# Turned maxima copied by ScalarE instead of VectorE, and the second mask product cut to its 64 non-zero columns

## The reference, cut to what matters

```
q, k, v = proj(wq), proj(wk), proj(wv)      # 32 heads of width 16
q, k = rope(q), rope(k)
scores = q @ k.T / sqrt(16)
scores = where(causal, scores, -inf)
attn = softmax(scores)                      # over the keys
out = attn @ v                              # then @ wo
```

## Time and profile before

| what | value |
|---|---|
| median of 3 runs | 857.84 us (856.75 to 858.73) |
| profiled execution, its span (no other time is shown for it) | 855.8 us |
| PE, DVE, ACT, POOL busy | 92%, 74%, 50%, 36% of the span |
| maxima (line 1614) | x320, 182.7 us busy on DVE |
| copies of the turned rows (line 1621) | x16, 402 ns median |
| mask products (line 734) | x512, 59.0 us busy on PE |
| attention with both kinds of scores | about 438 to 642 us of the span |

### The profile page before, as it was taken

One profiled execution on the slowest core, in us unless ns is written; L12 is line 12 of the kernel. 1 busy time (PEld: TensorE's weight loads), 2 busy tenths in 40 slices (PEclk: granted clock), 3 DMA queues, 4 the chain that ended last, 5 costly groups with the idle time before them and its releaser, 6 DMA issues.

```text
span 855.8 us, 18987 instructions
## 1 busy us (share of the span) xinstructions
PE 790.1 (92%) x7930; PEld 377.1 (44%) x7930; DVE 633.1 (74%) x895; ACT 427.9 (50%) x576; POOL 304.4 (36%) x217
## 2 busy tenths in 40 slices
PE   7668797797999999999989999999998999999997
PEld 2434343444444444544434444444435544444444
DVE  4999999998555333444569999999976787774344
ACT  4986557554844330143225777787784633332100
POOL 0699899993003000055530222212233222221000
PEclk9599899999999999999979999999998999999999
DMA  6900000005230000056640000000132023320001
GB/s 217 375 3 2 3 3 3 3 3 172 99 108 10 1 0 1 1 80 118 121 76 2 2 2 1 2 2 2 48 131 64 1 79 127 130 84 0 13 37 50
DMA packets 53297, 46.63 MB, mean 54 GB/s; under 512 B 38290, under 2 KB 44242, under 8 KB 53219
## 3 DMA queue, kind: packets, MB, share of 16 engines
q1 hardware_dynamic: 53218, 45.49, 18.6%
HBM read 34.87 MB, written 2.16 MB: 43 GB/s over the span
## 4 chain that ended last, share of the span: by engine, by line
PE 69%; DVE 16%; issue 5%; POOL 5%; ACT 3%; DMA 1%; SPq 1%; DVEq 0%; POOLq 0%; ACTq 0%
PE ps L870 13%; PE ps L651 10%; PE ps L628 8%; DVE arena L1388 8%; PE ps L805 8%; PE ps L906 7%; PE ps L730 6%; PE ps L707 6%; PE ps L789 3%; POOL arena L1238 3%; DVE arena L1614 2%; PE ps L734 2%; PE ps L542 2%; PE ps L498 1%; ACT arena L1147 1%
## 5 line engine op out<-in xcount | busy, mean ns | idle before, releaser
L1614 DVE TENSOR_REDUCE arena<-ps 128x1 f16<-128x512 f32 (+3 forms) x320 | 182.7, 630 | 11.1 <-PE ps L730 4.9
L1147 ACT ACTIVATE arena<-ps 128x1024 f32<-128x1024 f32 (+2 forms) x160 | 142.2, 942 | 54.4 <-PE ps L789 53.6
L1238 POOL TENSOR_TENSOR arena<-arena 128x1024 f32<-128x1024 f32 x62 | 152.0, 2487 | 9.4 <-DVE arena L1388 8.9
L1388 DVE TENSOR_TENSOR_SCAN arena<-arena,ps 128x1024 f32<-128x1024 f32 x64 | 142.0, 2268 | 1.4 <-PE ps L542 1.1
L870 PE MATMUL ps<-arena 128*128 128x512 f16 x528 | 114.6, 379 | 0.1
L730 PE MATMUL ps<-arena 64*128 64x512 f16 (+3 forms) x384 | 100.0, 337 | 4.5 <-DVE arena L1614 1.8
L651 PE MATMUL ps<-arena 128*128 128x512 f16 (+1 forms) x464 | 97.6, 372 | 1.0 <-ACT arena L1071 1.0
L1288 POOL TENSOR_SCALAR_AFFINE_SELECT arena<-arena 128x512 f32<-128x512 f32 x64 | 42.5, 669 | 155.4 <-ACT arena L1147 155.3
L996 ACT ACTIVATE arena<-arena,negA 128x1024 f32<-128x1024 f32 x64 | 72.9, 1147 | 45.4 <-DVE arena L1388 43.6
L542 PE MATMUL ps<-arena 64*128 64x64 f16 x3072 | 60.6, 196 | 35.8 <-DVE arena L1388 32.1
L542 PEld LDWEIGHTS ps<-arena 64*128 64x128 f16 x3072 | 52.8, 99 | 86.3 <-DVE arena L1388 79.3
(11 more groups left out here) (173 smaller groups left out, 964.6 us busy)
## 6 DMA issues: line engine op xcount, KB each, us to landing
arena<-in_w_q_dram SPq DMA_DIRECT2D x11, 768.0 KB, 4.3
arena<-c_rows SPq DMA_DIRECT2D x16, 512.0 KB, 11.2
arena<-in_w_s_dram SPq DMA_DIRECT2D x11, 384.0 KB, 4.8
arena<-in_x_fm_dram SPq DMA_DIRECT2D x8, 256.0 KB, 4.1
out_dram<-arena SPq DMA_DIRECT2D x8, 256.0 KB, 2.0
arena<-in_wg_dram SPq DMA_DIRECT2D x1, 1792.0 KB, 10.0
arena<-in_wu_dram SPq DMA_DIRECT2D x1, 1792.0 KB, 7.3
arena<-in_wd_dram SPq DMA_DIRECT2D x1, 1792.0 KB, 11.3
```

Of the source, the lines that this page charges most:

```text
L1147: nc.scalar.activation(dst, src, ACT.Exp, scale=float(HD) ** -0.5).then_inc(exp_done, 1)
L1238: nc.gpsimd.tensor_tensor(hC[i % 4][:], hst[i % 3][:], c_all[:, n, :], ALU.mult).then_inc(hc_done, 1)
L1388: nc.vector.tensor_tensor_scan(hst[i % 3][:], dA[i % 3][:], banks(2 * (i % 2), 2), 0.0, ALU.mult, ALU.add).then_inc(scan_done, 1)
L1614: nc.vector.reduce_max(maxima_slot(half, k), ps[:, ring_bank(n), 0:len(heads) * w].rearrange("p (a w) -> p a w", a=len(heads)), AX, negate ...
```

## The change

ScalarE takes over `keep_rows`, under a count of its own, `rows_kept`. `ring_read` then counts only what VectorE reads, so every wait on it is renumbered (`read_to`), and TensorE's wait for a bank whose last unit was a turn is a wait on `rows_kept`. The second mask product runs over 64 columns instead of 128.

```diff
+        ROWS_AT = {EARLY_TURN} | {RING_AT[step] for step in IN_RING if step[0] == "turn"}
+        def read_to(n):
+            return n + 1 - sum(at <= n for at in ROWS_AT)
+        def rows_to(n):
+            return sum(at <= n for at in ROWS_AT)
...
             def put_rows(g, half):
-                sp.wait_ge(ring_read, RING_AT["turn", g, half] + 1)
+                sp.wait_ge(rows_kept, rows_to(RING_AT["turn", g, half]))
...
             def ring_slot(n):
-                if EARLY <= n < EARLY + RING:
-                    pe.wait_ge(ring_read, EARLY)
-                elif n >= EARLY + RING:
-                    pe.wait_ge(ring_read, n - RING + 1)
-                elif n >= 2:
-                    pe.wait_ge(ring_read, n - 1)
+                before = EARLY - 1 if EARLY <= n < EARLY + RING else n - 2 if n < EARLY else n - RING
+                if before in ROWS_AT:
+                    pe.wait_ge(rows_kept, rows_to(before))
+                elif before >= 0:
+                    pe.wait_ge(ring_read, read_to(before))
                 return ring_bank(n)
...
                     if diag:
-                        for s in range(2):
-                            last = nc.tensor.matmul(dst[:, w - P:w], picks_b[rows, s, :], mask_b[rows, s, :], start=False, stop=(s == 1))
+                        for s, cols in ((0, P), (1, SUB)):
+                            last = nc.tensor.matmul(dst[:, w - cols:w], picks_b[rows, s, :], mask_b[rows, s, P - cols:P], start=False, stop=(s == 1))
...
+            def keep_rows(g, half, n):
+                act.wait_ge(ring_full, n + 1)
+                if g:
+                    act.wait_ge(m_rows[half], 32 * g)
+                nc.scalar.copy(m_row[0:GH, half * HALF:(half + 1) * HALF], ps[0:GH, ring_bank(n), :].bitcast(f16)[:, 0:HALF]).then_inc(rows_kept, 1)
             for t in range(TT):
                 stack(t)
+                if t == 5:
+                    keep_rows(0, 0, EARLY_TURN)
...
                     e += 1
+                elif kind == "turn":
+                    keep_rows(g, half, RING_AT[kind, g, half])
                 elif kind == "keep":
                     keep_out(g, half)
...
-            def keep_rows(g, half, n):
-                dve.wait_ge(ring_full, n + 1)
-                if g:
-                    dve.wait_ge(m_rows[half], 32 * g)
-                nc.vector.tensor_copy(m_row[0:GH, half * HALF:(half + 1) * HALF], ps[0:GH, ring_bank(n), :].bitcast(f16)[:, 0:HALF]).then_inc(ring_read, 1)
...
-                elif kind == "turn":
-                    keep_rows(g, half, RING_AT[kind, g, half])
```

More of the change, by code:

```diff
@@ L182, in build @@
         m_joined, r_made = sem("m_joined"), sem("r_made")
+        rows_kept = sem("rows_kept")
         m_rows = [sem("m_rows0"), sem("m_rows1")]
@@ L281, in searched @@
                 return len(SEARCH[0])
-            return max([RING_AT["search", g, half, k] for k in range(len(SEARCH[half])) if ("search", g, half, k) in RING_AT],
-                       default=EARLY - 1) + 1
+            return read_to(max([RING_AT["search", g, half, k] for k in range(len(SEARCH[half])) if ("search", g, half, k) in RING_AT],
+                               default=EARLY - 1))
+        ROWS_AT = {EARLY_TURN} | {RING_AT[step] for step in IN_RING if step[0] == "turn"}
[3 more added lines that the diff above has]
+            return sum(at <= n for at in ROWS_AT)
         def ring_bank(n):
@@ L834, in _ @@
                     turn_out(g, half, RING_AT[kind, g, half])
-            pe.wait_ge(ring_read, EARLY + len(IN_RING))
+            pe.wait_ge(ring_read, read_to(EARLY + len(IN_RING) - 1))
             for t in range(TT):
@@ L1131, in keep_out @@
                 if g:
-                    act.wait_ge(ring_read, RING_AT["out", g - 1, half] + 1)
+                    act.wait_ge(ring_read, read_to(RING_AT["out", g - 1, half]))
                 nc.scalar.copy(o_raw[:, half * HALF:(half + 1) * HALF], banks(7, 1)).then_inc(o_kept, 1)
@@ L1615, in maxima @@
                                      AX, negate=True).then_inc(ring_read, 1)
-            def keep_rows(g, half, n):
-                dve.wait_ge(ring_full, n + 1)
-                if g:
-                    dve.wait_ge(m_rows[half], 32 * g)
-                nc.vector.tensor_copy(m_row[0:GH, half * HALF:(half + 1) * HALF], ps[0:GH, ring_bank(n), :].bitcast(f16)[:, 0:HALF]).then_inc(ring_read, 1)
             def early(n):
-                if n == EARLY_TURN:
-                    keep_rows(0, 0, n)
-                else:
+                if n != EARLY_TURN:
                     maxima(*EARLY_UNITS[n], n)
@@ L1652, in divide @@
                                         ALU.mult).then_inc(ring_read, 1)
-                dve.wait_ge(ring_read, n + 1)
+                dve.wait_ge(ring_read, read_to(n))
             def nibbles(m, u, loads):
```

## The result

The changed kernel takes 861.11 us (median of 9 runs, 859.73 to 863.64), the kernel before 857.57 (9 runs, 855.56 to 860.84): a ratio of 1.0045, 95% interval 1.0029 to 1.0060, so 3.9 us slower (2.5 to 5.1). The forecast was 4.8 us slower.

What follows compares the result with a forecast made beforehand. VectorE was taken to set the pace in the attention, TensorE following through three banks. Terms +7.1 - 0.5 - 0.8 - 1.0 = +4.8 us, added to 857.8, gave 862.6 us, range 856.2 to 867.

Steps and rivals of the forecast that it cites:

- The copy leaves VectorE: All 16 turns: copies lie in the shadow of TensorE filling the next bank; removal gains 0.5 us, bounds 0 and 5.3.
- turn (7, 0): Group 7, half 0: next maxima start right behind VectorE's copy, so removing it gains 0.3 us.
- turns (0, 1) and (1, 0): Two turns where removing VectorE's copy was taken to gain 0.2 us together.
- Late release: ScalarE's copy queues behind exponentials, so TensorE's third search behind a turn starts late: +7.1 us with the last turn.
- half-0 turns: Turns (2, 0) to (6, 0): VectorE's maxima of the third search late by 0.92 us each, 4.6 for five.
- half-1 turns: Turns (3, 1), (4, 1) and (5, 1): VectorE late by 0.54 us each, 1.6 for three.
- the rival with double payment: Refilling the ring after a stall costs another 0.4 us at each of eleven turns: 867 us, chance 0.14.
- the turns (1, 1), (2, 1) and (6, 1): Exponentials stand otherwise there; each late by between nothing and 0.54 us, 0.5 taken for the three.
- The last turn: Turn (7, 1): no search follows, but ScalarE's exponentials run without a gap, so the copy adds 0.4 us.
- The early turn: Turn (0, 0): copy on ScalarE no longer waits for VectorE's rotary factors; gain 0.8 us, between 0 and 0.8.
- The narrower product: Second mask product over 64 fewer columns: 1.0 us faster, between 0 and 6.9, since VectorE paces most searches.
- The fast rival: VectorE's relief counts in full because rows are out before the bank is wanted: 851.5 us, chance 0.11.

Runs made afterwards that it cites:

- e4: The kernel before, with VectorE's copy of the turned rows cut to 32 of 512 columns (measuring only): 1.2 us faster than before, ratio 0.9986.
- e3: The changed kernel with ScalarE's copy one step earlier in its list, except at turns (0,1), (1,0) and (7,1): 0.3 us slower than the kernel before.
- e5: The changed kernel with ScalarE's copy cut to 32 of 512 columns (measuring only): 0.4 us faster than the kernel before, ratio 0.9995.
- e8: The changed kernel with ScalarE's copy one step ahead, as in e3, and cut to 32 of 512 columns (measuring only): 3.1 us faster than the kernel before.
- e9: e3 with the same bytes copied as 256 numbers of 4 bytes: 1.5 us faster than the kernel before, ratio 0.9982.
- e10: Changed kernel; VectorE copies half-0 turns of groups 1 to 6 and (7,1), ScalarE the rest as 4-byte numbers, mostly one step ahead: 2.8 us faster than before.
- e6: The changed kernel with ScalarE copying at turn (0,0) alone and VectorE at the other 15 turns: 2.2 us faster than the kernel before, ratio 0.9974.
- e1: The kernel before with the narrower second mask product alone, the copy staying on VectorE: 1.7 us faster than before, ratio 0.998.
- e7: The changed kernel with half-0 turns of groups 1 to 7 back on VectorE: 0.3 us faster than the kernel before, ratio 0.9997.
- e2: The changed kernel with the second mask product back at 128 columns, so ScalarE's copy alone: 6.9 us slower than the kernel before, ratio 1.008.

## Why the prediction was right

**The copy leaves VectorE for next to nothing: right.** e4 shows it: 3.0 us less work for VectorE gave 0.2 us. The 0.3 forecast at turn (7, 0) did show at first: its first maxima came 0.33 nearer to before. The 0.2 for turns (0, 1) and (1, 0) did not: together they lost 0.1.

**Late release: right in place, mechanism and size.** The forecast 0.92 at half-0 turns measured 0.89 at (5, 0), and the others of the five are alike; 0.54 at half-1 turns measured 0.43. The copy's price, taken from the row with 16 partitions, was 0.58 and measured 0.56. The `keep_out` and the exponentials behind the copy had the room that I gave them: at these eight turns nothing was lost beyond the third bank, which was the point of the rival with double payment. That rival fell. The later transfer of the rows cost nothing either: in the trace after, one `keys` step waits for it, 0.8 us at turn (7, 1), and its products start 4.62 us later than before (633.75 against 629.13), as bank 345 does. Of the turns (1, 1), (2, 1) and (6, 1), 0.5 forecast for the three, only (2, 1) lost anything, 0.28; the other two gained 0.1 each.

**Turn (7, 0): wrong.** I put it among the gains, from the copy's cover alone, and overlooked that the copy there stands behind `keep_out`:

```profile
617.06 0.59 ACT L1151 COPY arena<-ps 128x512 f32<-128x512 f32 x1
617.53 0.57 ACT L1140 COPY arena<-ps 4x512 f16<-4x512 f16 x1
...
618.15 0.39 PE L740 MATMUL ps<-arena 64*128 64x512 f16 x1
618.47 1.06 PE L815 MATMUL ps<-arena 128*32 128x512 f32 x8
619.47 0.39 PE L740 MATMUL ps<-arena 64*128 64x512 f16 x1
```

The third search starts 4.62 us later than before (613.53), where the maxima just ahead of the turn were 4.29 later. VectorE doesn't feel it yet, but the `values` step behind it is late by as much, and so is the fourth search (614.85 before): its maxima stand 0.51 further behind than those of the third. The turn lost 0.33 where I had booked a gain of 0.3.

**The last turn: wrong.** I added 0.4 us for the copy in ScalarE's full stretch; it cost nothing. There was a gap that I had not booked, ahead of the exponentials that begin at 629.62 before and at 634.25 after, 4.63 later, where bank 345 was 4.62 later:

```profile
629.62 2.86 ACT L1147 ACTIVATE arena<-ps 128x1024 f32<-128x1024 f32 x3 [0.48 <-PE ps L789]
...
634.25 2.85 ACT L1165 ACTIVATE arena<-ps 128x1024 f32<-128x1024 f32 x3 [0.28 <-PE ps L799]
```

(Before, and after.) Between bank 345 and the last out the distance even fell by 0.40. That goes with the clock and not with the copy. In the trace before, the granted clock falls from 1.00 to 0.50 some 1.07 us ahead of the last out. In the traces where the last out still finds the clock at 1.00 (the change, e3, e5, e8, e9, e10) the distance fell by 0.40 or 0.41, in e10 too, where VectorE copies the rows of turn (7, 1). Where the clock fell 0.95, 1.35, 2.45, 3.07 and 3.48 us ahead of it (e6, e1, e7, e4, e2), the distance changed by -0.05, 0.06, 0.25, 0.39 and 0.55.

**The early turn: right.** 0.8 was forecast. The distance went from 0.13 ahead of the turn to -0.28 with the second bank behind it and about -0.7 with the third. In the chain the second search behind the turn starts at 421.52, against 422.23 in the earlier trace rows.

**The narrower product: right within its interval.** 1.0 was forecast, 1.7 (0.2 to 3.3) measured; the trace has 0.8 in the steady part, where 0.5 was forecast, for products on which VectorE waits.

**The sum.** 4.8 forecast, 3.9 measured (2.5 to 5.1). The large terms hold by themselves; that the small ones come out as close is in part luck, since 0.9 us missed at turns (7, 0), (0, 1) and (1, 0) stand against 0.4 booked for nothing at the last turn and about as much at (1, 1), (2, 1) and (6, 1). The fast rival (851.5) needed ScalarE free before the turn; e3 made the release timely and still did not get there, so VectorE's relief had no 5 us in it.

## What to carry to other kernels

An engine at 98% in a ring of three banks need not be the one whose time counts: look whether the next bank was already full when it could have started. When a copy that frees a buffer moves to an engine with a quarter of its time free, look at that moment and not at the share: what stands ahead of it in the new engine's list, and how many banks it has before the producer stops. Moving it ahead in the list took back most of the loss here (3.6 of 3.9 us), but where there was no gap it handed about half of the delay on to what it overtook (0.46 of 0.95 us at turn (5, 0)). To be faster than before it took a shorter copy besides, or leaving alone the turns that have no gap.

## What the runs showed that I had not expected

The stretch at the lower of TensorE's two clocks where the attention starts differed between executions: the mean granted clock of 438 to 452 us was 0.51 of full speed before and 0.63 in e1, both between stretches at 1.00.

```profile
438.00:452.00 14.00, 12.08 (x66) 4.11 (x66) 8.40 (x15) 4.37 (x5) 1.90 (x3) 0.51 0.31 57
```

```profile
438.00:452.00 14.00, 11.46 (x60) 3.78 (x59) 9.41 (x17) 4.37 (x5) 2.75 (x5) 0.63 0.42 76
```

(Before, and e1.) It is not the edit that decides: the mean granted clock of 436 to 454 us was 0.62 before, in the change and in e7, and 0.72 in the other nine, and in all of these nine the distance to before fell by 1.0 to 1.4 us at that place, in the change and in e7 by 0.5. A difference of 1 us between two profiled executions of this kernel therefore says little. Distances taken between banks 43 and 345, behind that stretch, repeat to about 0.2 us: in e1 and e6, which are the same program there, they are -0.8 and -0.6.
